# A GRU, attention, Runge-Kutta and FFN kernel: four banks for the value products, FFN loads queued behind the drives, a hand order for the last three FFN tiles

## The reference, cut to what matters

```python
# 1: GRU over the 64 tokens, started from cond; hs are its states
r = sigmoid(i_r + h_r); z = sigmoid(i_z + h_z); n = tanh(i_n + r * h_n)
h = (1 - z) * n + z * h
# 2: attention, 16 heads of 128, one shared key and value head, causal, rotary
xn = layernorm(hs) * gamma
q, k, v = heads(xn @ Wq), xn @ Wkv[:, :128], xn @ Wkv[:, 128:]
x1 = x + softmax(mask(rot(q) @ rot(k).T)) @ v @ Wo
# 3: 64 Runge-Kutta steps (four stages each) driven by x1, from cond
dq = q - q**3 / 3 - p + drive + tanh(q) @ coupling.T + bias
dp = 0.08 * (q + 0.7 - 0.8 * p)
q = q + 0.01 / 6 * (dq1 + 2*dq2 + 2*dq3 + dq4)     # p the same, both clipped
# 4: FFN on the q of every step, 8-bit rows with a scale per row
t = silu(qx @ Wgate.T) * (qx @ Wup.T)              # 1408 columns, both rounded
out = x1 + quantized(t) @ Wdown.T
```

## Time and profile before

| | us |
|---|---|
| median of 3 runs | 1581.16 |
| lowest, highest | 1580.62, 1585.36 |
| the profiled execution | 1583.37 |
| its span, first to last instruction | 1581.6 |
| PE busy in it | 1493.9 (94%) |
| DVE busy | 1067.5 (67%) |
| ACT busy | 589.1 (37%) |
| POOL busy | 474.6 (30%) |

### The profile page before, as it was taken

One profiled execution on the slowest core, in us unless ns is written; L12 is line 12 of the kernel. 1 busy time (PEld: TensorE's weight loads), 2 busy tenths in 40 slices (PEclk: granted clock), 3 DMA queues, 4 the chain that ended last, 5 costly groups with the idle time before them and its releaser, 6 DMA issues.

```text
span 1581.6 us, 45959 instructions
## 1 busy us (share of the span) xinstructions
PE 1493.9 (94%) x16649; PEld 933.0 (59%) x16690; DVE 1067.5 (67%) x3437; ACT 589.1 (37%) x1917; POOL 474.6 (30%) x673
## 2 busy tenths in 40 slices
PE   5999999998899999999999999999999999999985
PEld 1333333334775758576767664766666666666662
DVE  1666766775764545464555552578999999899986
ACT  2444444553021020202020112455565566555552
POOL 0212121111220202020211110245566555656650
PEclk9999999998999999999999999999999999999997
DMA  8121122214300000000000105011111111111111
GB/s 309 45 51 48 45 53 60 65 39 148 42 1 7 20 12 14 27 0 27 0 27 0 27 5 213 26 29 40 34 37 34 49 45 33 37 33 37 35 46 39
DMA packets 91139, 72.68 MB, mean 46 GB/s; under 512 B 32824, under 2 KB 83000, under 8 KB 89912
## 3 DMA queue, kind: packets, MB, share of 16 engines
q1 hardware_dynamic: 71256, 59.09, 12.6%
q10 hardware_dynamic: 18048, 6.89, 1.7%
q0 software_dynamic: 1760, 5.77, 1.3%
HBM read 54.76 MB, written 16.94 MB: 45 GB/s over the span
## 4 chain that ended last, share of the span: by engine, by line
PE 71%; DVE 19%; issue 4%; ACT 4%; DMA 1%; SPq 0%; DVEq 0%; POOLq 0%; POOL 0%; ACTq 0%
PE ps L767 14%; PE ps L665 11%; PE ps L677 11%; PE ps L737 10%; PE ps L875 9%; DVE mem L1429 3%; PE ps L806 3%; DVE mem L1480 3%; PE ps L830 3%; ACT mem L1117 2%; DVE ps L1456 2%; PE ps L891 1%; DVE mem L1604 1%; DVE mem L1470 1%; DVE mem L1612 1%
## 5 line engine op out<-in xcount | busy, mean ns | idle before, releaser
L875 PE MATMUL ps<-mem 128*32 128x128 f32 x8192 | 277.9, 276 | 28.0 <-ACT mem L1117 18.5
L875 PEld LDWEIGHTS ps<-mem 128*32 128x32 f32 x8192 | 210.5, 110 | 102.3 <-ACT mem L1117 70.1
L582 POOL TENSOR_TENSOR mem<-mem 128x256 f32<-128x256 f32 x128 | 92.9, 726 | 450.3 <-DVE mem L1338 450.3
L767 PE MATMUL ps<-mem 128*128 128x256 f32 x1024 | 222.3, 379 | 0.0
L767 PEld LDWEIGHTS ps<-mem 128*128 128x128 f32 x1024 | 193.9, 190 | 26.0
L665 PE MATMUL ps<-mem 128*32 128x384 f32 x2048 | 181.8, 497 | 9.6 <-DMA mem<-in_W_ih 5.8
L677 PE MATMUL ps<-mem 128*32 128x384 f32 x2048 | 177.6, 487 | 2.4 <-DVE mem L1258 2.4
L737 PE MATMUL ps<-mem 128*128 128x512 f32 x384 | 168.7, 592 | 0.0
L1075 ACT ACTIVATE mem<-mem 128x512 f32<-128x512 f32 x32 | 19.7, 630 | 386.8 <-DVE mem L1370 386.8
L1117 ACT ACTIVATE mem<-mem 128x64 f32<-128x64 f32 x512 | 110.3, 250 | 90.6 <-DVE mem L1429 84.8
L865 PE MATMUL ps<-mem 128*128 128x128 f32 x768 | 137.5, 302 | 1.6
(11 more groups left out here) (152 smaller groups left out, 2172.1 us busy)
## 6 DMA issues: line engine op xcount, KB each, us to landing
mem<-x_scr SPq DMA_DIRECT2D x127, 64.0 KB, 1.8
mem<-in_xT SPq DMA_DIRECT2D x64, 64.0 KB, 1.9
mem<-in_Wq SPq DMA_DIRECT2D x1, 4096.0 KB, 12.5
mem<-in_Wo SPq DMA_DIRECT2D x1, 4096.0 KB, 15.3
q_scr<-mem SPq DMA_DIRECT2D x64, 64.0 KB, 1.6
mem<-q_scr SPq DMA_DIRECT2D x64, 64.0 KB, 1.9
out<-mem SPq DMA_DIRECT2D x64, 64.0 KB, 1.6
mem<-in_W_ih SPq DMA_DIRECT2D x1, 3072.0 KB, 10.0
```

Source lines behind the costliest of these rows:

```text
L582: pool.tensor_tensor(one, one, turned[h % 2].rearrange("p (b t) -> p b t", t=T), ALU.add).then_inc(qr_done, 1)
L767: mm = pe.matmul(ps[:, h % Q_BANKS, 0:BLK], wq[:, c, h * DH:(h + 1) * DH], xnb[:, c, :], start=(c == 0), stop=(c == NC - 1))
L875: mm = pe.matmul(ps[32 * j:32 * j + 32, st % 2, 0:P], thT[:, c, :], ct[:, c, j * P:(j + 1) * P], start=False, stop=(c == NC - 1), skip_gro ...
```

## The change

- **Values.** `PV_BANKS` gets a fourth bank, 4. Calls 0 to 3 of a block wait for no copy; call n from 4 on waits for the copy of call n-4. DVE waits for all copies before it writes `bias_ps` to bank 4.
- **SP's order.** The own drives, the store of the last rows, the drives 1 to 3 and the late rows of x stand ahead of all FFN loads.
- **Drive sum.** In step 0 the sum for step 1 stands at the fourth stage instead of the first.
- **ACT.** A Silu of one column stands behind the last copy of attention. ACT's groups are wrapped in a loop of one turn (`nought` is 0).
- **Tables.** The first chunk of product 5 goes from slot 0 to slot 1. Block 7 puts four heads instead of five ahead of the Runge-Kutta part; the late pieces take other slots (five instead of four in every fourth, none in (1, 9) and (2, 10)). The partial residual of block 6 goes from slot (2, 13) to (2, 14).
- **Tail.** The groups 16 to 18 are gone; every engine has a function `tail` with its own order for the tiles y, a and z = 13, 14 and 15. POOL takes the output add of y and the adding and rounding of the first part of a. PE's down product of z goes to bank 2, its first five passes ahead of the turn of z's second part.

```diff
-PV_BANKS = (5, 2, 3)
+PV_BANKS = (5, 2, 3, 4)
 GU_SLOTS = {...
-            0: ((4, 0, NC), (5, 0, 1)), 1: ((5, 1, NC),), 3: ((6, 0, NC),), 4: ((7, 0, NC),)}
+            0: ((4, 0, NC),), 1: ((5, 0, NC),), 3: ((6, 0, NC),), 4: ((7, 0, NC),)}
+LAST_BANK = 2
-EARLY_HEADS = {6: 8, 7: 5}
-LATE_SLOTS = (3, 2, 1, 4)
+EARLY_HEADS = {6: 8, 7: 4}
+LATE_SLOTS = (3, 2, 1, 5)
...
-                            if n >= 3:
+                            if n >= 4:
-                                pe.wait_ge(ao_cp, 4 * PAIRS * blk + n - 2)
-                            pe.matmul(ps[:, PV_BANKS[n % 3], :], vtok[...], pT[...],
+                                pe.wait_ge(ao_cp, 4 * PAIRS * blk + n - 3)
+                            pe.matmul(ps[:, PV_BANKS[n % 4], :], vtok[...], pT[...],
...
             act.wait_ge(ao_cp, 4 * PAIRS * NBLK)
+            act.activation(sig[1][:, 0:1], identf[:, 0:1], ACT.Silu)
...
+            dve.wait_ge(ao_cp, 4 * PAIRS * NBLK)
             dve.tensor_scalar(bias_ps, biasq, -ALPHA / BETA, None, ALU.add)
...
-                elif not end:
+                if not end and st == (0 if t else 3):
                     drive_sum(t + 1, (s + 1) % 4, g + 1 + (s == 3))
...
+            def tail():            # PE
+                y, a, z = LAST
+                product(a, 4, 0, NC)
+                product(a, 5, 0, NC)
+                t_turned(y, 1)
+                product(a, 6, 0, NC)
+                product(a, 7, 0, NC)
+                downs(y, 7)
+                x_turned(z)
+                pe.wait_ge(f_qTcp, z + 1)
+                for order in range(2 * GU_T):
+                    product(z, order, 0, NC)
+                t_turned(a, 0)
+                t_turned(a, 1)
+                downs(a, 7)
+                t_turned(z, 0)
+                pe.wait_ge(f_gated, GU_T * z + GU_T)
+                pe.wait_ge(f_tTcp, 2 * z + 1)
+                down(0, T_PARTS[0][1] // P, LAST_BANK)
+                t_turned(z, 1)
+                pe.wait_ge(f_tTcp, 2 * z + 2)
+                down(T_PARTS[0][1] // P, IC, LAST_BANK)
...
+            def tail():            # POOL
+                y, a, z = LAST
+                gate_scaled(a, 2)
+                gate_scaled(a, 3)
+                output(y)
+                for m in range(GU_T):
+                    gate_scaled(z, m)
+                lo, hi = T_PARTS[0]
+                pool.wait_ge(f_te, 1)
+                pool.tensor_tensor(vt[:, lo:hi], vt[:, lo:hi], et[:, lo:hi], ALU.add).then_inc(f_ta, 1)
+                t_rounded(a, 0)
```

More of the change, by code:

```diff
@@ L1172, in slot, with group @@
                         t_kept(i, 1)
-            def group(g, rk, tile):
+            def group(g, tile):
                 for k in range(16):
-                    if rk:
-                        stage(4 * g + k // 4, k // 4, k % 4)
+                    t = 4 * g + k // 4
+                    stage(t + nought if isinstance(g, int) and t > 0 else t, k // 4, k % 4)
                     if isinstance(g, int) and (g, k) == (0, 0):
```

279 lines of the change are left out of this document (185 added, 94 removed).

## The result

| | before | after |
|---|---|---|
| median (4 runs each) | 1582.39 us | 1559.91 us |
| lowest to highest | 1580.62 to 1585.36 | 1558.07 to 1560.21 |
| the profiled execution | 1583.37 | 1560.21 |
| its span | 1581.6 | 1558.4 |

The ratio of after to before is 0.9854, 95% interval [0.9835, 0.9872]: faster by 1.5%. Five more runs of the changed kernel in a later session gave 1558.15 (1557.87 to 1559.66) against 1582.76, a ratio of 0.9843 [0.9824, 0.9861]. The forecast was 1555.7 with a range of 1549 to 1567. The span fell by 23.2 us where the sum said 25.5.

A forecast was written before the change was run, and what follows sets the result against it. PE was taken to bound the kernel (71% of the wait chain, DVE 19%). Terms 12.4 + 6.4 + 0.6 + 0.4 + 5.7 = 25.5 us, taken from the 1581.16 median, gave 1555.7, range 1549 to 1567.

The forecast's parts named there:

- A: Attention values: a fourth bank lets calls three and four run together, saving 0.92 us per `values`, 12.4 in all.
- Rival 2: Attention values: the third call keeps the fourth from starting for another reason; gain about 1, time 1567 us; chance 0.05.
- B: Runge-Kutta entry: earlier first drive sum 3.0, second drive sum moved 1.9, PE's clock kept 1.5; 6.4 us together.
- The clock's 1.5: Entry: less PE idle time keeps the clock up, so two stages lose 1.55 us extra waiting; taken as 1.5.
- So I price the lateness at nothing: FFN loads moved behind the drives: 7 us of cover before step 4's drive sum, so their lateness costs 0.
- C: Single Runge-Kutta stages: earlier table load 0.45, moved residual add up to 0.35, filler costing up to 0.3; 0.6 us.
- D: Runge-Kutta loop: one product chunk moved from slot 0 to slot 1 saves 0.4 us over 13 groups.
- E: Tail: earlier gate parts, work given to POOL and five passes ahead of the second turn save 5.7 us.
- The 1567.5: Tail: the end time in us if PE's last passes run at the 2.4 GHz level, taking half the time.
- the estimate of 1.0 for filled waits: Tail: other tile's steps fill DVE's waits between gate parts, bringing its row scale 1.0 us earlier, beside 4.3.
- Rival 3: Tail: POOL is slow beside DVE, ends at 1559.5 and delays DVE's rounding; time 1558.3 us; chance 0.13.
- One sign of being wrong: Tail: the forecast called itself wrong if PE there waits for POOL's rounding; no size given.

The follow-up runs named there:

- experiment 1: Kernel before with only the fourth value bank and its later waits added: 1569.49 us, beside 1585.95 for the kernel before.
- experiment 2: Changed kernel with four banks, but value calls waiting for the same copies as in the kernel before: 1573.6 us, beside 1585.95 for the kernel before.
- experiment 3: Changed kernel with SP's order of before, all FFN loads ahead of the own drives: 1563.34 us.
- experiment 9: Changed kernel with the drive sum for step 1 back at the first stage of step 0: 1560.09 us, beside 1582.76 for the kernel before.
- experiment 11: Changed kernel with down-weight loads alone behind the drives, 24 unused PE products in the tail, DVE replacing POOL for tile 14's first add: 1554.52 us, ratio 0.9819.
- experiment 10: Changed kernel with 8 and 16 unused matrix products in PE's two idle stretches of the tail: 1557.75 us, beside 1580.79 for the kernel before.
- experiment 6: Changed kernel with DVE's two grid steps for tile 14's second part moved directly behind those of its first part: 1556.34 us.
- experiment 4: Changed kernel with the FFN loads two steps later, behind the second step's store and next drive: 1559.49 us.

## Why the prediction was right, and where its steps were off

**A, 12.4 forecast, 13.3 measured** (experiments 1 and 2). The mechanism is shown from both sides: banks alone give all of it, the wait alone takes it back. The loop calls gained 0.94 (10.75 to 9.81 us between the two `values` of block 1) against 0.92. The excess: 0.4 over the twelve loop calls, 0.1 in block 0, and 0.35 in the last block, where 0.2 was set and its two `values` with what follows took 8.14 us instead of 8.69. Rival 2's other reason doesn't exist.

**B, 6.4 forecast, 6.3 measured at the entry.** The landing took 1.3 us, at the low end of the 1.1 to 2. The order is worth 5.3 in experiment 3, the drive sum 2.2 in experiment 9, and the two overlap. The clock's 1.5 is a term of the first trace more than of the kernel: with the loads ahead it fell in all four traces, but the excess of the first two slots there was 0.1, 0.3, 0.6 and 1.5 us. That the sum met the 6.3 so closely is partly luck: the profile it was read from has the longest entry of its kind, and against the two others (29.1 and 29.8) the changed entries are 4.4 to 5.7 us shorter.

**The step that failed** is the sentence "So I price the lateness at nothing". It named as users of the queue the drive of step 4 and the FFN weights, gave them 7 us of cover, and that cover held: no wait for either shows. A third user was not named, PE's own instructions. In that stretch they come by DMA while it runs, and beside 6 MB of data a block came up to two stages late. The cost is 2.05 us in the first profile, and 0 to 3.2 in the seven traces of this order, so it also makes the kernel's time less steady. Before, the same loads ran beside the last projection, 32 long passes on a few instructions: one packet of queue 8 came in it, at 964.53, and the next only at 986.46, behind the loads.

**C and D, 1.0 forecast together, 1.1 measured** (steps +0.9 with 2.05 of long slots in it). The slots show each term: (1,13) 2.70 to 2.22, (2,13) 2.56 to 2.26, (1,9) 2.38 to 2.21, slot 0 2.31 to 2.16, slot 1 2.13 to 2.25. Against them seven slots with five pieces cost 0.07 each, 0.5 in all, where I had up to 0.3.

**E, 5.7 forecast, 5.5 measured, for the wrong reasons.** Between the two old tails (45.4 and 46.1) and the nine changed ones (38.9 to 40.8) the gain is 4.6 to 7.1 us, so the close match is luck too. The last rounding was to come 5.7 us earlier and came 3.5 earlier. The clock was taken at the lower level for the last passes, and was at the upper, which gave about 2 us back. (The 1567.5 that the prediction names for the upper level doesn't follow from its row: halving eleven passes of 0.43 gives 2.4 us, so 1568.6.) What failed first was the row scale, 5.3 earlier by the sum and 3.4 in the trace: the estimate of 1.0 for filled waits left out that DVE's steps get longer beside POOL's new ones. Rival 3 had the pair right and was half right on who pays. POOL's add took 1.85 us and its rounding 1.73, near its 1.55 to 1.84, and it ended 22.8 us behind the last stage, between the forecast's 21.2 and the rival's 24.0; DVE paid more, 1.77 for a step of 0.56. One sign of being wrong did show: PE waits 4.32 us for POOL's rounding. It didn't hold up PE's passes by itself, since it then waits 1.95 us more for DVE's rounding of the same tile. The path behind it was missing from the sum: PE came back from these waits at the 1.2 GHz level, its eleven passes of tile 14 took over 4 us instead of 2.85 (experiment 11), and the end hung on them and no longer on the last rounding. By experiments 10 and 11 the clock is worth up to 2.1 us in the tail and 1.1 more behind the later idle stretch, and giving POOL's add back to DVE 0.4.

**The rest, +0.9,** is the part ahead of A, which no edit touches. Over the fourteen traces it lies between 436.0 and 437.9 us; where the time goes isn't settled (from 20 to 50 us the granted clock is 0.94 before and 0.89 after, from 425 to 437 us 0.86 and 0.78). A forecast made from one profiled execution carries that much by itself.

The sum came out 2.3 us too large against the spans: 2.05 for the fetches, 0.9 for the start of the run, 0.2 for the tail, less 0.9 that A gave more; B, C and D cancel.

## What to carry to other kernels

Two calls that can share PE's array should have a result bank each and no wait between them: the array was half empty for want of one of eight banks, and one line gave 13 us. When a bulk load is moved in a queue, list all that will be fetched while it runs, the instruction blocks of unrolled code among them; it is free beside long passes and not beside many short instructions. A step given to an idle engine is not free if it slows the busy engine beside it: look at what the busy engine does then. And compare a stretch over several traces before you credit an edit: the same tail took 38.9 to 40.8 us here, enough to make a loss look like a gain (experiment 6).

## What the runs showed that I had not expected

- DVE's step on 768 columns with one input takes 0.56 us alone, and 1.77 and 1.78 when POOL adds two arrays of 640 columns beside it; with the same step in another place it was 0.56 again. Where they meet, DVE's step ends some 0.4 us behind POOL's: 1537.45 + 1.77 = 1539.2 behind 1536.96 + 1.85 = 1538.8. The Trainium skill, "GPSIMD Engine Reference", Specifications, says that POOL shares its SBUF interfaces with VectorE, with contention for VectorE's instructions in a 2-port mode or with two SBUF inputs. The trace agrees for the second form (DVE's add of two inputs took 1.76 us beside POOL's rounding in experiment 6, 0.96 alone), and adds that DVE can be the one that waits; whether the grid step is in such a mode no row shows.
- After an idle stretch of PE the granted clock fell in some traces and not in others of equal order: with 2.4 us of idle (1524.3 to 1526.7) it fell to 0.55 in the changed kernel's first profile and in five more traces of the same tail, and stayed at 1.00 in three (experiments 2, 4 and 9). With that stretch filled it stayed at 1.00 in both kernels that did so; behind the later idle stretch it fell in one of them (2.0 us of idle) and held in the other (1.8 us).
- Instruction blocks delayed by data traffic stop PE with no semaphore to show for it, only "issue": in six of seven traces with the loads behind the drives, in none of the seven with the loads elsewhere.
